# Waits ahead of 23 prologue gathers in place of 6, in a deformable-convolution kernel

## The reference, cut to what matters

```
x = x + conv(LN_channels(x))               # x: (4, 64, 32, 32)
    offset = conv3x3(n, offset_w) + b      # 18 channels: 9 taps, y and x
    mask   = sigmoid(conv3x3(n, mask_w))   # 9 channels
    val    = bilinear(n at tap + offset) * mask     # 4 corners per tap
    out    = einsum('bcthw,oct->bohw', val, weight)
    out    = silu(batchnorm(out))
t = tokens(x)                              # (4, 1024, 64)
t = t + sum over 4 branches of w_r * stu(LN(t)[:T/frac])
    stu: causal convolution of u with 16 filters phi (1024 long), plain and
    with alternating signs, mixed by M_phi_plus, M_phi_minus, and 3 lags by M_u
```

## Time and profile before

| | us |
|---|---|
| median of 3 runs | 618.11 |
| lowest, highest | 615.82, 621.09 |
| the profiled execution's own time | 615.08 |
| its span, first to last instruction | 613.2 |
| PE busy | 466.6 |
| DVE busy | 308.9 |
| POOL busy | 291.0 |
| ACT busy | 226.2 |

### The profile page before, as it was taken

How to read it: one execution, slowest core, us unless ns; L and a number is a source line. 1 busy time by engine, 2 the same in 40 slices (tenths; PEclk the granted TensorE clock), 3 DMA queues, 4 the chain that set the end, 5 groups by cost and what they waited for, 6 DMA issues and landing times.

```text
span 613.2 us, 8001 instructions
## 1 busy us (share of the span) xinstructions
PE 466.6 (76%) x3022; PEld 256.5 (42%) x3022; DVE 308.9 (50%) x762; ACT 226.2 (37%) x515; POOL 291.0 (47%) x295
## 2 busy tenths in 40 slices
PE   4967559645666787699879996676678758998996
PEld 3522331422453444345435553444244424554543
DVE  5638752229996365637463746383636363612000
ACT  1126430015433453343434334433344334443432
POOL 1057747470374666466646664755476637000000
PEclk9877767558777898799989998877688969999999
DMA  7925933390132332233313321322133212100000
GB/s 156 177 78 166 339 103 103 96 342 18 36 91 64 87 90 83 64 92 94 86 55 95 87 85 55 100 78 77 56 92 95 86 48 92 33 1 1 10 0 10
DMA packets 43631, 53.95 MB, mean 88 GB/s; under 512 B 24536, under 2 KB 34014, under 8 KB 43593
## 3 DMA queue, kind: packets, MB, share of 16 engines
q0 software_dynamic: 13824, 37.77, 20.7%
q1 hardware_dynamic: 23745, 13.42, 8.5%
q10 hardware_dynamic: 6024, 2.26, 1.7%
HBM read 50.12 MB, written 3.30 MB: 87 GB/s over the span
## 4 chain that ended last, share of the span: by engine, by line
PE 49%; DVE 15%; issue 12%; another core or an unknown queue 10%; ACT 10%; DMA 2%; POOL 1%; SPq 1%; ACTq 0%; DVEq 0%
PE bank L1017 20%; PE bank L978 7%; ACT u_conv L739 6%; PE bank L852 5%; PE bank L1026 3%; PE bank L915 3%; PE bank L833 2%; PE bank L905 2%; DVE G L490 2%; DVE sil L503 2%; PE bank L882 1%; PE bank L862 1%; DMA filt<-in_L_ffn_phi_dram 1%; PE bank L824 1%
## 5 line engine op out<-in xcount | busy, mean ns | idle before, releaser
L296 POOL DMA_INDIRECT G<-corner_table,idx x288 | 288.4, 1001 | 231.4 <-issue 75.3
L1017 PE MATMUL bank<-filt,u 128*128 128x512 f16 (+1 forms) x960 | 206.9, 364 | 3.1 <-ACT u_conv L739 3.0
L739 ACT COPY u_conv<-bank 64x512 f32<-64x512 f32 x256 | 148.5, 580 | 160.4 <-PE bank L1017 60.7
L1017 PEld LDWEIGHTS bank<-filt,u 128*128 128x128 f16 x960 | 93.8, 102 | 104.4 <-issue 29.5
L490 DVE TENSOR_TENSOR G<-G,bank 128x2304 f32<-128x2304 f32 x32 | 81.6, 2551 | 73.2 <-DMA G<-corner_table,idx 71.4
L978 PE MATMUL bank<-u_conv,mixw 128*64 128x256 f32 (+1 forms) x640 | 71.1, 357 | 9.1 <-issue 8.8
L978 PEld LDWEIGHTS bank<-u_conv,mixw 128*64 128x64 f32 x640 | 43.1, 144 | 31.2 <-issue 21.4
L1026 PE MATMUL bank<-filt,u 64*128 64x256 f16 x168 | 30.0, 287 | 29.3 <-ACT u_conv L739 29.1
L494 DVE TENSOR_TENSOR V<-G 128x576 f32<-128x576 f32 x32 | 24.3, 758 | 41.3 <-PE bank L906 27.6
L491 DVE TENSOR_TENSOR G<-G 128x1152 f32<-128x1152 f32 x32 | 43.4, 1358 | 1.1
L502 DVE TENSOR_SCALAR expo<-expo 128x128 f32<-128x128 f32 x16 | 4.0, 250 | 70.1 <-ACT expo L706 51.8
(11 more groups left out here) (174 smaller groups left out, 425.6 us busy)
## 6 DMA issues: line engine op xcount, KB each, us to landing
filt<-filter_rows SPq DMA_DIRECT2D x16, 514.0 KB
G<-corner_table,idx POOLq DMA_INDIRECT x288
corner_table<-n_uT SPq DMA_DIRECT2D x12, 128.0 KB, 3.5
mixw<-in_x_dram SPq DMA_DIRECT2D x2, 512.0 KB, 6.2
filt<-in_L_ffn_M_phi_plus_dram SPq DMA_DIRECT2D x4, 256.0 KB
out_dram<-o_sb ACTq DMA_DIRECT2D x8, 128.0 KB, 2.2
filt<-n_L_ffn_M_phi_minus_dram ACTq DMA_DIRECT2D x2, 256.0 KB
corner_table<-n_uT ACTq DMA_DIRECT2D x4, 128.0 KB, 4.4
```

The costliest lines, as they stand in the source:

```text
L296: pool.indirect_dma_start(G[:, k, tap, :], None, corners[bp], bass.IndirectOffsetOnAxis(ap=idx[:, q % 2, k, tap:tap + 1], axis=0)).then_in ...
L739: act.copy(u_conv[C * par:C * par + C, g % 2, :, b2, p, :], conv_ps[b2][rows].rearrange("c (k a) -> c k a", k=GROUP)).then_inc(conv_copied ...
L1017: last = pe.matmul(out_of[b2][:, :, a0:P], u16[:, NJ * bp + j2, hl, b2, par:par + 2].rearrange("s w c -> s (w c)"), filt_h[:, ks, par, par ...
```

## The change

In `keep_pace` the waits ahead of six gathers of q 0 and q 1 give way to waits ahead of 23 (21 conditions, of which the last holds at three gathers). Each makes POOL wait, ahead of the gather named, until a semaphore of the prologue has reached a count. In q 0 the wait for `off_turned` 2 at gather 9 stays, and the three for `mats_summed` 4, 6 and 8 at gathers 20, 25 and 30 become one for 2 at gather 14 and one for 7 at gather 26. In q 1 the wait for `n_turned` moves from gather 4 to gather 0, and the one for `off_turned` from gather 20 to gather 13. All others are new. No instruction is added but waits, and q 2 and later are as they were.

```diff
--- before.py
+++ after.py
@@ -271,14 +271,50 @@
                 step, last = (STEPS * (q - 1) + STEPS * (m - LEAD) // (BLK * TAPS) for m in (i, i - 1))
                 if q >= 2 and (step != last or i == 0):
                     pool.wait_ge(conv_done[step % 2], step // 2 + 1)
-                if q == 0 and i == TAPS:
-                    pool.wait_ge(off_turned, 2)
-                if q == 0 and i in (20, 25, 30):
-                    pool.wait_ge(mats_summed, (i - 15) // 5 * 2 + 2)
-                if q == 1 and i == 4:
-                    pool.wait_ge(n_turned, 8)
-                if q == 1 and i == 20:
-                    pool.wait_ge(off_turned, 2 * BP)
+                if q == 0:
+                    if i == 3:
+                        pool.wait_ge(n_turned, 4)
+                    if i == 9:
+                        pool.wait_ge(off_turned, 2)
+                    if i == 11:
+                        pool.wait_ge(x_turned, 4)
+                    if i == 14:
+                        pool.wait_ge(mats_summed, 2)
+                    if i == 17:
+                        pool.wait_ge(f_rows_ready, 1)
+                    if i == 20:
+                        pool.wait_ge(v_ready[0], START + 1)
+                    if i == 23:
+                        pool.wait_ge(pixels_scaled, 1)
+                    if i == 26:
+                        pool.wait_ge(mats_summed, 2 * BRANCHES - 1)
+                    if i == 28:
+                        pool.wait_ge(v_ready[1], START + 1)
+                    if i == 30:
+                        pool.wait_ge(n_ready, 3)
+                    if i == 33:
+                        pool.wait_ge(w_turned, 1)
+                if q == 1:
+                    if i == 0:
+                        pool.wait_ge(n_turned, 8)
+                    if i == 3:
+                        pool.wait_ge(y_convolved, 1)
+                    if i == 7:
+                        pool.wait_ge(off_done, 3)
+                    if i == 10:
+                        pool.wait_ge(off_done, 4)
+                    if i == 13:
+                        pool.wait_ge(off_turned, 2 * BP)
+                    if i == 15:
+                        pool.wait_ge(v_ready[1], START + 2)
+                    if i == 17:
+                        pool.wait_ge(val_turned, START + 2)
+                    if i == 20:
+                        pool.wait_ge(y_convolved, 2)
+                    if i == 23:
+                        pool.wait_ge(u_ready, 2)
+                    if i >= 27 and i % 3 == 0:
+                        pool.wait_ge(conv_done[1], (i - 24) // 6 + 1)
 
             for bp in range(BP):
                 for q in range(4 * bp, 4 * bp + 4):
```

## The result

The changed kernel takes 597.96 us in the median of five runs (593.63 to 604.94), beside 615.82 us (610.13 to 621.09) of the kernel before. The ratio is 0.9696, with a 95% interval of 0.9642 to 0.975: 17.9 us less, where 11.0 were forecast. The forecast time was 607.1 us, in a range from 598 to 617, so the result lies at the range's lower edge, just outside it. The profiled execution took 601.72 us, its span is 599.8 us. Some executions of either kernel are slower than the rest by 1.5% or more, and all ratios in this document leave these out.

The account below looks back on a forecast made before the run. Long runs of POOL gathers were taken to hold back PE's completions. A middle prologue gain of 12.3 us less 1.3 for late gathers made 11.0, so 618.1 - 11.0 = 607.1 us, range 598 to 617.

Parts of the forecast that it names:

- gather 33: q 0's wait for `w_turned`: POOL's pause releases the first transposes at 79.0 to 80.0, 4.2 to 5.2 us earlier.
- the price of the waits in q 1: Pauses charged in q 1: 5.7 to 8.7 us together at gathers 7, 10 and 13, up to 4.7 each later.
- the third place: PE's second value convolution, taken late by ACT beside gathers and filter loads: 6.7 us gained to 3.1 lost.
- L852 was to start at 83.8 to 84.8: Offset matmuls of the second pair on PE, to start then instead of at 88.97, after an earlier q 1.
- the forecast's own mechanism: Long runs of gathers hold PE's completions back; they come 1.9 to 2.9 us after POOL stops.
- the opening of the main loop: Gathers 23 to 35 of q 1 move behind `u_ready` 2 and end late: 1.3 us lost, 0 to 4.0.
- the slower rival: Thirteen gathers run through in the main loop's opening and PE crawls: 14 us lost, ending at 624 to 632; chance 0.10.
- The loads hold the signals as well: Filter loads also hold PE's signals, so only the second place, the offset matmuls, gains: 611 to 617 us; chance 0.14.
- Nothing is freed: PE is late for its own reason, such as its clock; time stays at 618, between 615 and 622; chance 0.15.
- the mixing weights were to be scaled near 130 us: Sign of being right: DVE's scaling at the prologue's end starts near 130, where it was 142.73.
- ACT's unknown releases ahead of the mixing weights: Sign of being right: their share before DVE's scaling of those weights falls by more than half.
- The first gather of q 2: Sign of being wrong: its interval from `u_ready` 2, 18.5 us before, grows by several us.

Follow-up runs that it names:

- f4: Kernel before, with gather 20 of q 1 also waiting for `u_ready` 2, so POOL is quiet while the filters load; ratio 1.004.
- e4: Changed kernel without the waits at gathers 7, 10 and 13 of q 1 (`off_turned` back at gather 20); ratio 0.977 to the kernel before.
- e5: Changed kernel without the waits from gather 17 of q 1 on; ratio 1.000 to the kernel before.
- g4: Changed kernel without the waits at gathers 27, 30 and 33 of q 1; 592.53 us, ratio 0.975 to the kernel before.
- g1: The changed kernel measured once more on another chip, with nothing altered; 594.4 us, ratio 0.976 to the kernel before.
- g3: Changed kernel with `u_ready` 2 awaited at gather 20 of q 1 in place of `y_convolved` 2; 597.3 us, ratio 0.982 to the kernel before.
- f1: Kernel before, with gathers 0 to 19 of q 1 fetching only 64 of 256 floats per row; 620.06 us in one run.
- f2: Kernel before, with gathers 3 to 19 of q 1 left out and memsets keeping POOL busy instead; 604.73 us in one run.
- e1: Kernel before with the change's new waits in q 0 only, q 1 keeping its old ones; ratio 0.997.

## Why the prediction was right in kind and off in size

**Right.** An unbroken run of gathers holds PE's results back and a pause frees them. With POOL pausing ahead of gather 33, the first weighed value came at 80.02, for which 79.0 to 80.0 was forecast. The loads by themselves hold nothing (f4: 0.04 us).

**The term that failed** is the price of the waits in q 1. The working charged each of the waits at 7, 10 and 13 with a pause of 1.9 to 2.9 us, 5.7 to 8.7 together, and the third place with four gathers and pauses of up to 4.7 us each. Measured was 2.86 us at 7 and nothing at 10 and 13, 2.47 at 17 and nothing at 20. It is no accident of this profile: in all eleven profiles with the three waits at 7, 10 and 13, one or two of them made a pause, 1.9 to 4.7 us together, and the one at 13 never did. After one break PE runs ahead of POOL, so that its next signals are there before the next wait is reached. The offsets came at 103.92, 14.7 us earlier (forecast 7.0 to 13.9), and from there to the mixing weights 18.9 us went by in place of 24.1: 5.1 gained, where the bounds were 6.7 gained and 3.1 lost and the middle of 1.8 gained was taken. With one pause of 1.9 to 2.9 us in place of three, the same working puts the offsets at 100.9 to 102.9 (82.7 or 83.7, plus 16.3 and the pause), 15.8 to 17.8 us earlier. That is more than the 14.7 measured; the late start told below took some of it back. e4 and e5 show these two terms apart: 6.5 us at the mixing weights for the first three waits, the whole gain for the later ones. e5 also shows how little the terms add up, since an early gain is lost again if a long run follows it.

**Missed, the other way:** L852 was to start at 83.8 to 84.8 and started at 88.38. Gathers 33 to 35 and those of q 1 up to gather 6 follow without a pause from 80.25 on, the forecast's own mechanism, and they held `y_convolved` 1 until 87.66. The wait for it at gather 3 of q 1 made no pause: ACT had the count at 87.66, POOL came to that gather at 88.16. The delay cost time at the offsets. In the ten profiles with the changed kernel's code up to gather 16, these 72 matmuls start at 83.49 to 90.02 us, and the last offsets follow 14.5 to 17.0 us later: 83.52 and 99.52 in g4, 88.38 and 103.92 here. So two errors of opposite sign met in this term, and that it came out only 0.8 us above its upper bound is in part luck.

**Right in size:** the opening of the main loop. It was to cost 1.3 us (0 to 4.0) and cost 1.2 in the changed kernel and 2.3 in g1, against before. The way to it was another, though: the 1.3 us were reckoned from late gathers with three pauses in them, and the waits at 27, 30 and 33 made no pause. It was the unbroken run of 13 that the slower rival spoke of, and ACT had one late release in it, at 143.22. The rival's crawl exists, only not at 13 gathers: in 18 unbroken ones PE crawls, and the opening costs 5.2 us (g3) to 9.4 us (f4) more than before.

**The other rivals.** "The loads hold the signals as well" fell with f4. "Nothing is freed" fell with the result. The Trainium skill's "SBUF — State Buffer", § "Who interferes with whom", says that DMA never contends with a compute engine and that PE and ACT wait on nobody. No run here looks at the memory ports, and they may well be free. But what a reader takes from it, that gathers cannot slow PE's results, does not hold here: ACT waited 24.49 us in e5 for a result 21.9 us old, and the 72 matmuls took 25.2 us beside unbroken gathers and 10.93 at nearly the same clock with a pause among them.

**Of what was to be seen,** the mixing weights were to be scaled near 130 us and were at 122.86. L852 took 10.93 us where 12 to 15 were forecast. ACT's unknown releases ahead of the mixing weights fell from 43.4 us to 25.5, by 41% and not by more than half. The first gather of q 2 came 21.1 us after the mixing weights, 2.6 more than before.

## What to carry to other kernels

Where an engine stands idle for a signal whose sender is long done in the trace, look for a long run of indirect DMAs from POOL beside it, and break that run where a result on the path is due; a wait for that very result costs a pause only when the result is really held. Don't break by count or by the gathers' own landing: that frees as much, but the gathers themselves come late, and it costs where the next engine stands for them. Move no more of them behind the break than the next stretch can cover, and look at that stretch again. Take more than one profile before reading a difference of a few us at a mark as an effect.

## What the hardware showed that was not expected

Results of PE come late beside running indirect DMAs whatever their bytes (256 or 64 floats in a row, the same crawl in f1), and not beside a POOL that is busy otherwise (f2). The delay grew to 21.9 us within 26 gathers (e5), with filter loads beside them, and was 3.5 us within the ten from 80.25 on. The matmuls can crawl, too: 0.9 us each (17.2 / 19) at a granted clock of 0.55, where they take 0.14 us at full clock and 0.16 at 0.64 (e4, 11.52 / 72). What sets the crawl off is open. It began after 53 of the 72 matmuls in the kernel before, after 44 in f1 and after 67 in e1, and in e4 not at all within 14 unbroken gathers.

Which resource it is, was not found. Signals of ACT pass at once in the same gathers (87.93 to 87.98), so a queue that all engines' signals share does not fit; a path that only PE's signals take, or the DMA engines' work on a gather's descriptors, would both look like this, and no kernel here tells them apart. The profile models the ends of matmuls, so it does not say either whether a late result was finished and its signal held, or whether its last part was really late.
